# A graph kernel builds its edge matrices in groups of 14 destinations instead of 16, and GpSimd makes two of six weighted one-hots

## The reference, cut to what matters

```python
agg = segment_sum(x[src], dst, num_segments=n)                        # layer 0, no weights
msgs = x[col] * vals[:, None]; agg = segment_sum(msgs, row, n)        # layer 2, here row=src, col=dst as given
```

## Time and profile before

| what | value |
|---|---|
| time, median of 3 runs | 2250.18 us (2249.29 to 2251.86) |
| the profiled execution's own time | 2255.12 us |
| its span | 2252.7 us |
| mean granted TensorE clock | 0.971 |
| busy share of the span | PE 96%, PEld 84%, DVE 68%, ACT 49%, POOL 24% |
| the stage of the change, first to last adjacency matmul | 16 to 151 us of the span |

### The profile page before, as it was taken

How to read it: one execution, slowest core, us unless ns; L and a number is a source line. 1 busy time by engine, 2 the same in 40 slices (tenths; PEclk the granted TensorE clock), 3 DMA queues, 4 the chain that set the end, 5 groups by cost and what they waited for, 6 DMA issues and landing times.

```text
span 2252.7 us, 30357 instructions
## 1 busy us (share of the span) xinstructions
PE 2157.4 (96%) x10594; PEld 1892.4 (84%) x10594; DVE 1540.0 (68%) x2661; ACT 1096.2 (49%) x2052; POOL 544.1 (24%) x986
## 2 busy tenths in 40 slices
PE   7889988669899999999999999999999999999999
PEld 7889985459678888888888888888888888888888
DVE  7772647453577777777677777777677777777665
ACT  5683335343454555544454455554454455554443
POOL 0010000120122333223322233223322233223320
PEclk9889997789999999999999999999999999999999
DMA  2001002340011111111111111111111111111111
GB/s 64 1 1 45 31 6 98 126 125 1 29 43 41 54 43 38 39 55 43 38 38 43 57 38 38 43 48 47 43 39 38 57 43 38 38 47 52 38 38 55
DMA packets 71019, 101.32 MB, mean 45 GB/s; under 512 B 5847, under 2 KB 41255, under 8 KB 70871
## 3 DMA queue, kind: packets, MB, share of 16 engines
q1 hardware_dynamic: 67523, 93.70, 13.3%
q0 software_dynamic: 3040, 5.19, 0.8%
q10 hardware_dynamic: 308, 0.51, 0.1%
HBM read 91.64 MB, written 7.74 MB: 44 GB/s over the span
## 4 chain that ended last, share of the span: by engine, by line
PE 74%; DVE 0%; ACT 0%; DMA 0%; issue 0%
PE psum L651 24%; PE psum L652 24%; PE psum L653 24%; PE psum L2231 1%; PE psum L2124 0%; PE psum L2114 0%; DMA w_raw<-in_w 0%; DVE w_lo L2286 0%; ACT w_forms_hi L1966 0%; PE psum L2131 0%; ACT w_hi L1975 0%; DVE x_rows L2378 0%; ACT f_rows L645 0%; DVE x_rows L2410 0%; DVE stats L609 0%
## 5 line engine op out<-in xcount | busy, mean ns | idle before, releaser
L651 PE MATMUL psum<-w_hi,hidden_hi 128*125 128x512 f32 x1280 | 503.3, 393 | 2.5 <-issue 2.4
L653 PE MATMUL psum<-w_hi,hidden_lo 128*125 128x512 f32 x1280 | 504.7, 394 | 0.0
L652 PE MATMUL psum<-w_lo,hidden_hi 128*125 128x512 f32 x1280 | 504.6, 394 | 0.0
L652 PE MATMUL psum<-x_forms_lo,w_forms_hi 128*128 128x418 f32 x1260 | 445.3, 353 | 0.0
L2378 DVE SCALAR_TENSOR_TENSOR x_rows<-psum,leaf_by_token,x_rows 125x512 f32<-125x512 f32 x320 | 233.9, 748 | 254.2 <-PE psum L653 254.2
L2004 ACT ACTIVATE hidden<-psum 128x418 f32<-128x418 f32 x315 | 161.9, 514 | 487.1 <-PE psum L653 484.9
L1907 POOL TENSOR_TENSOR w_forms<-w_raw 128x128 f32<-128x128 f32 x189 | 104.8, 582 | 1128.4 <-PE psum L653 598.8
L651 PEld LDWEIGHTS psum<-w_hi,hidden_hi 128*125 128x125 f32 x1280 | 237.4, 185 | 59.3 <-issue 2.7
L653 PEld LDWEIGHTS psum<-w_hi,hidden_lo 128*125 128x125 f32 x1280 | 236.7, 185 | 59.0
L652 PEld LDWEIGHTS psum<-w_lo,hidden_hi 128*125 128x125 f32 x1280 | 237.1, 185 | 54.3
L2351 DVE TENSOR_TENSOR hidden_lo<-hidden,hidden_hi 128x418 fp32r<-128x418 f32 (+1 forms) x384 | 255.2, 691 | 21.2 <-ACT hidden_hi L2026 21.2
(11 more groups left out here) (364 smaller groups left out, 3439.4 us busy)
## 6 DMA issues: line engine op xcount, KB each, us to landing
w_raw<-in_w SPq DMA_DIRECT2D x127, 512.0 KB, 3.7
expert_raw<-in_experts SPq DMA_DIRECT2D x8, 1024.0 KB, 5.9
expert_results_d<-expert_results SPq DMA_DIRECT2D x16, 160.0 KB, 5.0
c_rows_d<-c_rows SPq DMA_DIRECT2D x10, 250.0 KB
x_rows<-in_x SPq DMA_DIRECT2D x5, 448.0 KB
W_raw<-in_gnn_W SPq DMA_DIRECT2D x4, 512.0 KB, 3.8
W_raw<-in_gnn_W SPq DMA_DIRECT2D x1, 2048.0 KB, 9.7
b_by_token<-in_b SPq DMA_DIRECT2D x8, 256.0 KB, 3.8
```

The costliest lines, as they stand in the source:

```text
L651: t.matmul(out, stat[0], mov[0], start=start, stop=False, skip_group_check=again)
L652: t.matmul(out, stat[0], mov[1], start=False, stop=False, skip_group_check=again)
L653: return t.matmul(out, stat[1], mov[0], start=False, stop=stop, skip_group_check=again)
```

## The change

Windows have 14 destinations: 90 windows of 140 columns, and 30 full sets. The window of a destination is no longer a shift by 4 but a multiplication and a shift, so one more instruction stands in the preparation on DVE. `LOAD` is 5, and on DVE that load stands between `L` and `E` instead of ahead of `L`. Of the six static weighted one-hots of a set, the last two are made by a new POOL program; DVE makes none, ACT four. DVE's wait for the end of `L`, which stood ahead of L405, goes with it.

```diff
-WIN = 16
+WIN = 14
-KEY = 256
+KEY = 16 * WIN
+WIN_MUL, WIN_SHIFT = 4682, 16
-    LOAD = 9
+    LOAD = 5
-    HERE = 1
+    HERE = 2
-            s.then(v.tensor_single_scalar(win_i[:, :], raw_i[:, 1, :], 4, ALU.logical_shift_right))
+            s.then(v.tensor_scalar(win_i[:, :], raw_i[:, 1, :], float(WIN_MUL), 0.0, ALU.mult, ALU.add))
+            s.then(v.tensor_single_scalar(win_i[:, :], win_i[:, :], WIN_SHIFT, ALU.logical_shift_right))
...
-                if n % LOAD == 0 and n:
-                    extra = load_extra(v, regs[n // LOAD % 2], n)
                 pairs = pairs_of(n)
...
+                if n % LOAD == 0 and n:
+                    extra = load_extra(v, regs[n // LOAD % 2], n)
                 shape = [EB, pairs, COLUMNS]
                 v.tensor_tensor(E[:, n % RING, 0:pairs], ...
-                if n == 0:
-                    v.wait_ge(pair_copied, WEIGHT_COPIED)
-                v.wait_ge(low_made, n + 1)
-                for q in range(pairs - HERE, pairs):
-                    w, u = n * SET + q // SLOTS, q % SLOTS
-                    v.tensor_scalar(LW[:, n % RING, q, :], L[:, n % RING, q, :], g.pair_w[:, w, u:u + 1], None,
-                                    ALU.mult).then_inc(weighted_here, 1)
...
+        @block.gpsimd
+        def _(q):
+            q.wait_ge(pair_copied, WEIGHT_COPIED)
+            for n in range(NSETS):
+                pairs = pairs_of(n)
+                q.wait_ge(low_made, n + 1)
+                if n >= RING:
+                    q.wait_ge(used, n - RING + 1)
+                for p in range(pairs - HERE, pairs):
+                    w, u = n * SET + p // SLOTS, p % SLOTS
+                    q.tensor_scalar(LW[:, n % RING, p, :], L[:, n % RING, p, :], g.pair_w[:, w, u:u + 1], None,
+                                    ALU.mult).then_inc(weighted_here, 1)
```

More of the change, by code:

```diff
@@ L233, in phase_adjacency @@
     weighted = sem("a_weighted")
-    weighted_here = sem("a_weighted_by_vector")
+    weighted_here = sem("a_weighted_by_gpsimd")
     used = sem("a_used")
```

## The result

The kernel with the change takes 2224.52 us (median of 4 runs, 2223.22 to 2225.95), the one before 2249.73 us (2247.31 to 2251.86) beside it: a ratio of 0.9888, 95% interval 0.9871 to 0.9906. The forecast was 2225.0 us, 2214 to 2239. The profiled execution took 2225.38 us with a span of 2223.6 us and a mean granted clock of 0.978; the one of before took 2255.12 us at 0.971. The number was right. The way to it was right in its main step, the second rounds, and wrong in which engine sets the pace and in what POOL costs it; two errors cancelled.

The account below looks back on a forecast made before the run. Sets with two rounds lost 30.4 us; without them DVE would barely set the pace. Thirty 3.32 us sets plus extras, 109.3 us, end the stage at 125.6 instead of 150.75: 25 off the 2250.2 median, 2225 us, range 2214 to 2239.

Parts of the forecast that it names:

- Step 1: Windows of 14: all 30 sets have one round, waits and clock falls go; plain PE set 2.87 us, at most 3.28.
- Step 2: DVE's plain set falls from 3.55 to 3.02 us, 3.40 at worst if 0.38 of register work stays uncovered.
- Step 3: POOL's two weighted one-hots run beside DVE and hold it up 0.30 us a set, ends 0 and 0.54.
- rival (b): POOL holds DVE for its whole instruction, 0.92 us a set instead of 0.30: 2243.7 us; chance 0.13.
- Step 4: Loads of five counts hold back DVE's L397 by about 0.3 us, five times: 1.5 us, ends 0 and 6.5.
- Step 5: ACT loses one L571 piece, its set 3.28 to about 2.97 us; the preparation's new instruction adds 0.4 us.
- rival (a): PE sets the pace, POOL's hold costs nothing, register work covered; stage ends 118.5 to 119, time 2218.5 us; chance 0.20.
- rival (c): PE's clock falls to 1.2 GHz for much of the stage; with half its work so, 2267 us; chance 0.05.

Follow-up runs that it names:

- 380-column run: The changed kernel with DVE's three column one-hots of a round computed 380 columns wider (520), output unchanged: 2241.46 us, ratio 0.9962, stage end 137.8 us.
- each wider run: Two runs of the changed kernel with a round's column one-hots on DVE made 130 or 380 columns wider: 2229.4 us and 2241.46 us.

## Why the prediction was right, and where it was not

**Step 1, the windows: right, and it carries the result.** 30 rounds, no second ones (30 loads of first blocks), no fall of the clock in the stage, a plain set of 2.93 us on PE where I took 2.87 and bounded by 3.28. The run with second rounds put back shows the cause by itself: by the medians all of the gain went with them.

**Step 2, DVE's set: right.** L408 follows L399 by 0.94 us, as forecast (0.95); the register work is covered, and the run without POOL shows what it costs uncovered, 0.2 us of idle in nearly every set.

**Step 3, POOL beside DVE: the mis-sized term.** I took 0.30 us a set, between 0 and 0.54, from POOL's two-input form beside a long DVE form. Measured are 0.06 (3.08 against the 3.02 of step 2) to 0.11 (the six one-hots with and without POOL). I had also taken POOL's instruction as 0.30 to 0.46 us; it is 0.59. What I had not asked is who is held: it is POOL, which starts behind L399 and loses some 0.8 us there (1.44 at most, 0.59 at least), and POOL has the time. The page "SBUF — State Buffer" of the Trainium skill (Who interferes with whom) says that a DVE instruction with two SBUF inputs contends with a GpSimd one that reads SBUF, that the lock is exclusive, and that issue order decides who is blocked. The trace agrees for the pair that I feared for in rival (b), with the parts the other way round: L399 is first, and POOL waits for the rest of its 0.95 us. For the round's one-hots it does not show a wait for POOL's whole 0.59 us, but 0.11 in each set, and in the tile sets with wider one-hots 0.1 on each of two and some 0.04 on each of two more.

**Step 4, the loads: too dear.** A load takes 1.18 us, 0.3 more than L388's 0.87, as I gave; but only one of the five holds DVE. Set 25 takes 3.35 us instead of 3.08, with 0.23 of idle before L408 (103.77 above), not before L399. Sets 5 and 10 take 3.10 and 3.64 like their neighbours: the load of set 5 begins at 30.2 us, 2.7 ahead of that set's L388. (Sets 15 and 20 lie where PE holds DVE.) So the term was some 0.3 us and not 1.5.

**Step 5: right on ACT** (2.85 for 2.97), wrong on the preparation: the new instruction takes its 0.29 us, but DVE's wait for the small constants behind it shrank from 1.07 to 0.53 us, and these came 0.27 us earlier than before; the first load of the counts takes DVE 0.85 us with five where it took 1.11 with nine. L388 of set 0 starts at 13.09, not 13.95. In set 1 DVE then waits 1.9 us for the vectors' transpose, which takes that back.

**The sum.** DVE's last one-hot ended at 117.4 instead of 123.2: 0.9 us from the start, 7.2 from POOL's price (30 x 0.24), 1.2 from the loads and 0.5 from the ten `bn_stats` (0.56 each); and back 1.9 from that wait in set 1 and about 2 from sets 14 to 24, in which PE holds DVE. Behind it PE needed 3.4 instead of 2.3 us, since PE, not DVE, had led the sets before. So the stage ended at 120.8 and not at 125.6. With that, the mechanism was nearer to rival (a), "PE sets the pace", which named 118.5 to 119; the runs make it a tie, in which PE leads the sets with tiles and gates and DVE the plain ones.

**Why the number came out all the same.** The stage gained 30 us and not 25 by the profiles, which would have given 2220. But the profiled execution of before was of the longer kind, 4.9 us above its median, and that of the change lies only 0.9 us above its own. I carried the 4.9 us over as if they belonged to the whole kernel. They do not: the runs of the kernel before show that they go with a lower mean clock, which the change's runs don't have, and likely with this stage. The two errors, 4.8 us in the stage's end and some 4 us in this distance, cancel. The median's gain of 25.2 us agrees with my 25 by that accident.

**The slower rival (c)** did not come about: PE's clock was 1.00 from 25 us to the stage's end, also in the 380-column run, where PE was idle for 12 of 112.8 us in pieces of at most 1.1 us (0.79 us in the last set).

## What to carry to other kernels

A second round that reuses a buffer of the first costs more than its work: here 5.7 us, of which the idle was 2.7, its own matmuls 1.0 and the clock behind it 2.1 on average; a slightly smaller tile that avoids it altogether pays, and the smaller step beside it (here POOL's, worth 0 with the second rounds and 10 us without) must be judged after it. When two engines come out within a few per cent of each other, don't ask which one leads in one kind of set: follow the lag between them through all sets, and compare its end with the least it can be. Before a forecast is set against a median, look at the profiled execution's clock beside that of the other runs: its distance from the median may go with the clock, and then need not survive the change.

## What the runs showed of the hardware that I had not expected

- POOL's product with one tensor input and one scalar for each partition, 125x128 f32, takes 0.59 us at least (60 of them); its two-tensor form of 128x128 took 0.46 at the median. On DVE the same instruction (L407) takes 0.28.
- When POOL and DVE's two-tensor L399 meet, POOL pays: up to 1.44 us for 0.59.
- DVE's 128-column one-hot goes at 0.20 us from start to start, and at 0.31 in some sets with POOL beside it (two of three in 14 of the 30 sets of each wider run: all ten tile sets and four plain ones; in the change twice in all). Which instruction of POOL must lie where for that is not settled; no run here moved POOL's start alone.
- Behind a single idle of 2.65 to 2.68 us PE's granted clock fell to 0.50 in three of four cases, for 10.2 us each in the kernel before and for 3.4 to 6.9 with the second rounds put back; with many idles of up to 1.1 us, 12 of 112.8 us together, it stayed at 1.00.
- Executions of the kernel before took 2253.6 to 2254.9 us at a mean clock of 0.971 and 2246.8 to 2250.9 at 0.973 to 0.976 (12 runs); those of the changed one lie within 3 us at 0.978 (4 runs).
